# Two attention layers with expert layers: f32r scores one head at a time become bf16 scores two heads at a time, in the two row halves of the array

## The reference

```python
s = jnp.einsum('bhqd,bhkd->bhqk', q, k) * scale      # 16 heads of 8 features
s = jnp.where(causal, s, -jnp.inf)                   # layer 0 only
p = jax.nn.softmax(s, axis=-1)
o = jnp.einsum('bhqk,bhkd->bhqd', p, v)
...
x = _layernorm(x + _L0_attn_ref(...))                # 16 heads, causal
x = _layernorm(x + _L0_ffn_ref(...))                 # 8 experts, top 2, relu
x = _layernorm(x + _L1_attn_ref(...))                # 16 heads, full
x = _layernorm(x + _L1_ffn_ref(...))                 # 15 experts, top 3, gelu, and a shared expert
```

## Time and profile before

| what | value |
|---|---|
| median of three runs | 1208.55 us |
| runs | 1205.19 to 1209.41 us |
| span of the profiled execution | 1058.9 us |
| outside the span, median less span | 149.65 us |
| mean granted clock of TensorE | 0.927 |
| PE, DVE, ACT, POOL busy | 906.3, 679.9, 549.4, 444.0 us |

### The profile page before, as it was taken

How to read it: one execution, slowest core, us unless ns; L and a number is a source line. 1 busy time by engine, 2 the same in 40 slices (tenths; PEclk the granted TensorE clock), 3 DMA queues, 4 the chain that set the end, 5 groups by cost and what they waited for, 6 DMA issues and landing times.

```text
span 1058.9 us, 23206 instructions
## 1 busy us (share of the span) xinstructions
PE 906.3 (86%) x7486; PEld 763.1 (72%) x7486; DVE 679.9 (64%) x2209; ACT 549.4 (52%) x1320; POOL 444.0 (42%) x688
## 2 busy tenths in 40 slices
PE   5899988995999996998999896899898999789910
PEld 4788878884899985766888665676666789688810
DVE  3467755673644475987655566888875565378863
ACT  1356654562655564666766474567556655334300
POOL 7000100054500075477200375325776157377774
PEclk9699998997999998999999897999989999989965
DMA  4557564555468433364667333323444789888421
GB/s 78 103 107 193 114 142 101 135 135 133 106 178 204 125 68 59 53 125 85 144 182 191 66 57 58 51 35 56 87 90 130 216 264 326 280 247 270 122 64 53
DMA packets 111752, 138.49 MB, mean 131 GB/s; under 512 B 12275, under 2 KB 86033, under 8 KB 111633
## 3 DMA queue, kind: packets, MB, share of 16 engines
q1 hardware_dynamic: 100241, 114.97, 45.9%
q0 software_dynamic: 10240, 20.99, 7.9%
q10 hardware_dynamic: 1152, 1.05, 0.6%
HBM read 70.25 MB, written 42.48 MB: 106 GB/s over the span
## 4 chain that ended last, share of the span: by engine, by line
PE 49%; DMA 20%; issue 8%; POOL 7%; DVE 7%; SPq 6%; ACT 2%; POOLq 0%; ACTq 0%; DVEq 0%
DMA QK<-parts 10%; PE bank_O L1132 5%; PE bank_N L1224 5%; DMA G<-yd,ypos 5%; PE bank_FH L1212 4%; POOL xs L877 4%; PE bank_S L1087 4%; PE bank_T L1110 3%; PE bank_S L1083 3%; PE bank_S L1085 3%; PE bank_T L1114 3%; SPq L736 2%; PE bank_T L1112 2%; PE bank_M L1056 2%; DMA QK<-mrow 2%
## 5 line engine op out<-in xcount | busy, mean ns | idle before, releaser
L1298 DVE TENSOR_REDUCE mp<-bank_S 128x3 f32<-128x384 f32 (+1 forms) x512 | 304.2, 620 | 133.9 <-PE bank_S L1087 91.7
L948 ACT ACTIVATE P<-bank_T 128x384 f32<-128x384 f32 (+1 forms) x512 | 260.9, 543 | 90.0 <-PE bank_T L1114 58.2
L891 POOL DMA_INDIRECT G<-yd,ypos x160 | 155.2, 970 | 76.1 <-issue 47.3
L877 POOL DMA_INDIRECT xs<-X,ypos x160 | 155.9, 974 | 48.7 <-issue 43.6
L1132 PE MATMUL bank_O<-P,V 128*32 128x256 f32 (+1 forms) x2048 | 128.8, 371 | 1.4 <-ACT P L948 1.0
L1083 PE MATMUL bank_S<-QK 96*128 96x256 f32 x512 | 112.4, 322 | 18.5 <-DMA QK<-parts 8.9
L1110 PE MATMUL bank_T<-QK 128*128 128x256 f32 x512 | 110.8, 322 | 10.6 <-ACT P L948 6.1
L828 POOL TENSOR_TENSOR rstd<-mv,half 128x2 f32<-128x2 f32 x48 | 9.6, 200 | 261.4 <-DVE mv L1351 261.1
L1085 PE MATMUL bank_S<-rmat 128*128 128x256 f32 x256 | 91.7, 358 | 22.3 <-DMA QK<-parts 21.6
L1083 PEld LDWEIGHTS bank_S<-QK 96*128 96x128 f32 x512 | 79.5, 201 | 35.8 <-DVE mp L1298 20.5
L1087 PE MATMUL bank_S<-QK 96*128 96x128 f32 (+1 forms) x512 | 104.7, 292 | 0.0
(11 more groups left out here) (171 smaller groups left out, 1753.3 us busy)
## 6 DMA issues: line engine op xcount, KB each, us to landing
QK<-parts SPq DMA_DIRECT2D x192, 128.0 KB
QK<-wtab SPq DMA_DIRECT2D x76, 257.0 KB, 3.9
W<-w_in SPq DMA_DIRECT2D x46, 321.0 KB, 4.0
QK<-xs SPq DMA_DIRECT2D x38, 256.0 KB, 4.3
yd<-P SPq DMA_DIRECT2D x38, 256.0 KB, 3.9
xs<-zeros SPq DMA_DIRECT2D x17, 512.0 KB, 8.1
xp<-xs SPq DMA_DIRECT2D x22, 256.0 KB, 4.1
yd<-yb SPq DMA_DIRECT2D x22, 256.0 KB, 4.0
```

Of the source, the lines that this page charges most:

```text
L877: pool.indirect_dma_start(xs[g % 2], bass.IndirectOffsetOnAxis(ypos[L][:, 2 * b + blk, k:k + 1], 0), X[:, 2 * b + blk, :], None).then_inc( ...
L891: pool.indirect_dma_start(G[i][:, blk, k, :], None, yd[g], bass.IndirectOffsetOnAxis(ypos[L][:, 2 * b + blk, k:k + 1], 0))\
L948: act.activation(P[:, (h // 4) % 2, h % 4, 0:n], bank[("T0", "T1")[h % 2]][:, 0:n], ACT.Exp, scale=SCALE)\
L1298: dve.tensor_reduce(mp[:, a % 2, 0:n, h], bank[("S0", "S1")[h % 2]][:, 0:n * w] .rearrange("p (a c) -> p a c", a=n), AX.X, ALU.max).then_i ...
```

## The change

**Three bf16 parts.** q and k are split into a high, a middle and a low bf16 part. `qk_lo` becomes `qk_rest` (DVE), `qk_mid` (ACT) and `qk_low` (DVE). A head's six products of parts take 6 x 8 = 48 rows, so a head fits into half of the array's rows. `spread_parts` writes `parts` to a DRAM buffer `stk` (one DMA), and `stack` reads from it into `QK` with six DMAs for all 16 heads. `QK` is bf16 and holds four attentions; before, its four slots held eight heads each.

**Pairs.** Even heads lie in rows 0 to 63, odd heads in rows 64 to 127. `scores` and `scores_T` issue the matmuls of two heads by turns, one in each row half, each half to a bank of its own. S0 and S1 are now filled together by one pair, and one `row_max` (two heads) frees both; the same for T0 and T1 with one `exp`. The mask is added with four bf16 matmuls of 64 rows for a pair.

**Bursts of eight.** `weigh_V` takes eight heads, four column groups with two heads each, summed in the same bank with 18 columns, of which nine are zero for each head. `O_T` has four transposes in place of eight. `max_neg`, `max_T` and `max_rows` work once for 16 heads in place of twice, and the maxima are split into three bf16 parts.

**Buffers and order.** P holds 16 heads; layer 1's pages store from the same ring of four as layer 0's. `PRM` has other numbers throughout, so that the order of all engines differs. `lay_out()` counts 0.1 more on PE whenever the kind of row or column grouping changes from one step to the next.

The core of the diff:

```diff
+TILING = {"scores": 1, "scores_T": 1, "weigh_V": 2}
+SWITCH = 0.1
...
-        QK = [sb(f"QK{i}", [D, NH // 2, 2, T], F32R) for i in range(4)]
-        VPAD = NH * VW + 32 - VW
-        V = [sb(f"V{i}", [D, 2, VPAD]) for i in range(3)]
-        P = sb("P", [D, 2, 4, 2 * T])
...
+        QK = sb("QK", [D, NQK, 2, NP, T], BF16)
+        V = [sb(f"V{i}", [D, 2, VW // 2 + NH * VW]) for i in range(3)]
+        P = sb("P", [D, PSLOTS, 2 * T])
...
-            def stack(a, u):
-                c = 2 * a + u
+            def spread_parts(a):
                 sp.wait_ge(lo_done.sem, lo_done.all(a))
-                if a < 2:
-                    sp.wait_ge(cleared.sem, 1 + 3 * c)
-                    if c == 0:
-                        sp.wait_ge(cleared_dve.sem, 2)
+                if a >= 2:
+                    sp.wait_ge(stacked[(a - 2) % NQK].sem, stacked[0].all((a - 2) // NQK))
+                sp.dma_start(stk[a % 2].rearrange("i p t -> p i t"), slots(parts[:, :, :, :])).then_inc(spread[a % 2].sem, DMA)
+
+            def stack(a):
+                sp.wait_ge(spread[a % 2].sem, spread[a % 2].all(a // 2))
+                if a < NQK:
+                    sp.wait_ge(cleared.sem, 2 * a + 2)
                 else:
-                    sp.wait_ge(st_ps.sem, st_ps.at(a - 2, 8 * u + 8))
-                p = parts[64 * u:64 * u + 64, :, :, :].bitcast(F32).rearrange("p s i t -> p (s i) t")
-                for i, pair in enumerate((p[:, 0::2, :], p[:, 0::3, :], p[:, 1:3, :])):
-                    sp.dma_start(QK[c % 4][HD * i:HD * i + HD, :, :, :].bitcast(F32), pair).then_inc(stacked[c % 4].sem, DMA)
+                    sp.wait_ge(st_ps.sem, st_ps.all(a - NQK))
+                parts_of = stk[a % 2].rearrange("i (d h) t -> i d (h t)", h=NH)
+                for lane in range(2):
+                    run = parts_of[:, :, lane * NP * T:(lane + 1) * NP * T]
+                    for row, n, src in ((0, 3, run.rearrange("i d c -> (i d) c").rearrange("(s r) c -> r s c", s=2)),
+                                        (3, 2, run.rearrange("(m i) d c -> (i d) m c", m=3)[:, 0::2, :]),
+                                        (5, 1, run.rearrange("i d c -> d i c")[:, 0::5, :])):
+                        at = lane * HALF + row * HD
+                        sp.dma_start(QK[at:at + n * HD, a % NQK, :, :, :].rearrange("r s h t -> r s (h t)"), src)\
+                            .then_inc(stacked[a % NQK].sem, DMA)
...
+            def qk_mid(a):
+                act.wait_ge(rest_done.sem, rest_done.all(a))
+                act.activation(slots(parts[:, :, :, :])[:, 1::3, :], rest[:, :, :], ACT.Copy).then_inc(mid_done.sem, 1)
...
+            def max_rows(a):
+                act.wait_ge(m_kept.sem, m_kept.all(a))
+                for lane in range(2):
+                    at = lane * HALF + QROWS
+                    act.dma_start(QK[at:at + 3, a % NQK, 0, :, :], mrow[3 * NP * lane:3 * NP * (lane + 1), a % 2, :])\
+                        .then_inc(m_stacked[a % NQK].sem, DMA)
...
+            def exp(a, p):
+                act.wait_ge(st_ps.sem, st_ps.at(a, p + 1))
+                if NH * a + 2 * p >= PSLOTS:
+                    _, before, u = before_pair(a, p)
+                    act.wait_ge(o_ps.sem, o_ps.at(before, u + 1))
                 n = 3 * D if a < NB else 2 * T
-                act.activation(P[:, (h // 4) % 2, h % 4, 0:n], bank[("T0", "T1")[h % 2]][:, 0:n], ACT.Exp, scale=SCALE)\
+                i = p_slot(a, 2 * p)
+                act.activation(P[:, i:i + 2, 0:n], pair["T"][:, :].rearrange("p (h c) -> p h c", h=2)[:, :, 0:n], ACT.Exp, scale=SCALE)\
                     .then_inc(exped.sem, 1)
...
+            def mask(banks, which):
+                for i in range(2):
+                    m = masks[which][i]
+                    n = D if which == i else HALF
+                    at = 0 if which == i or i == 0 else HALF
+                    for lane in range(2):
+                        rows = slice(lane * HALF, (lane + 1) * HALF)
+                        pe.matmul(diagonal(banks[lane])[:, :, at:at + n], pick[i][rows, :],
+                                  m[rows, :].unsqueeze(1).broadcast_to((HALF, 2, n)), start=(i == 0), stop=False,
+                                  skip_group_check=True)
+
+            def scores(a, p):
+                banks = free("S0"), free("S1")
+                if a == 0 and p == 0:
+                    pe.wait_ge(const_in.sem, CONST_LOADS * DMA)
+                if p == 0:
+                    pe.wait_ge(stacked[a % NQK].sem, stacked[a % NQK].all(a // NQK))
+                if a < NB:
+                    mask(banks, 0)
+                for qb, (o, n) in enumerate(((0, T), (T, T)) if a >= NB else ((0, D), (D, T))):
+                    for lane in range(2):
+                        rows = slice(lane * HALF, lane * HALF + QROWS)
+                        m = pe.matmul(banks[lane][:, o:o + n], QK[rows, a % NQK, 0, p, qb * D:(qb + 1) * D], QK[rows, a % NQK, 1, p, 0:n],
+                                      start=(a >= NB), stop=(a >= NB or qb == 1), skip_group_check=True)
                 m.then_inc(s_ps.sem, 1)
-                held[k] = maxed.sem, maxed.at(a, h + 1)
-
-            def max_T(a, u):
+                held["S0"] = held["S1"] = maxed.sem, maxed.at(a, p + 1)
...
+            def scores_T(a, p):
+                banks = free("T0"), free("T1")
+                if p == 0:
+                    pe.wait_ge(m_stacked[a % NQK].sem, m_stacked[a % NQK].all(a // NQK))
+                if a < NB:
+                    mask(banks, 1)
+                for kb, (o, n) in enumerate(((0, T), (T, T)) if a >= NB else ((0, T), (T, D))):
+                    for lane in range(2):
+                        rows = slice(lane * HALF, lane * HALF + QROWS + 3)
+                        m = pe.matmul(banks[lane][:, o:o + n], QK[rows, a % NQK, 1, p, kb * D:(kb + 1) * D], QK[rows, a % NQK, 0, p, T - n:T],
+                                      start=(a >= NB), stop=(a >= NB or kb == 1), skip_group_check=True)
                 m.then_inc(st_ps.sem, 1)
-                held[k] = exped.sem, exped.at(a, h + 1)
-
-            def weigh_V(a, g):
+                held["T0"] = held["T1"] = exped.sem, exped.at(a, p + 1)
...
                 for kb in range(2):
-                    for j in range(4):
-                        h = 4 * g + j
-                        w = V[a % 3][:, kb, h * VW:h * VW + 32]
-                        if a >= NB or kb == 0:
-                            o, x = O[32 * j:32 * j + 32, 0:T], P[:, g % 2, j, kb * T:(kb + 1) * T]
-                        else:
-                            o, x = O[32 * j:32 * j + 32, D:T], P[:, g % 2, j, T:T + D]
-                        m = pe.matmul(o, w, x, start=(kb == 0), stop=(kb == 1), skip_group_check=True)
+                    for lane in range(2):
+                        for j in range(BURST // 2):
+                            h = BURST * u + 2 * j + lane
+                            w = V[a % 3][:, kb, h * VW + (VW // 2 if lane == 0 else 0):][:, 0:VW]
+                            q = 0 if a >= NB else kb * D
+                            x = P[:, p_slot(a, h), kb * T:kb * T + T - q]
+                            m = pe.matmul(O[32 * j:32 * j + VW, q:T], w, x, start=(kb == 0 and lane == 0), stop=(kb == 1 and lane == 1),
+                                          skip_group_check=True)
                 m.then_inc(o_ps.sem, 1)
-                held["O"] = o_kept.sem, o_kept.at(a, g + 1)
-
-            def O_T(a, blk):
+                held["O"] = o_kept.sem, o_kept.at(a, u + 1)
...
+            def qk_low(a):
+                dve.wait_ge(mid_done.sem, mid_done.all(a))
+                p = slots(parts[:, :, :, :])
+                dve.tensor_tensor(p[:, 2:4, :], rest[:, :, :], p[:, 1::3, :], ALU.subtract).then_inc(lo_done.sem, 1)
+
+            def row_max(a, p):
+                dve.wait_ge(s_ps.sem, s_ps.at(a, p + 1))
+                if p == 0 and a >= 2:
+                    dve.wait_ge(mT_ps.sem, mT_ps.all(a - 2))
                 n, w = (3, D) if a < NB else (2, T)
-                dve.tensor_reduce(mp[:, a % 2, 0:n, h], bank[("S0", "S1")[h % 2]][:, 0:n * w]
-                                  .rearrange("p (a c) -> p a c", a=n), AX.X, ALU.max).then_inc(maxed.sem, 1)
-
-            def max_neg(a, u):
-                heads = slice(8 * u, 8 * u + 8)
-                top = mp[:, a % 2, 0:2, heads]
-                dve.wait_ge(maxed.sem, maxed.at(a, 8 * u + 8))
+                S = pair["S"][:, :].rearrange("p (r c) -> p r c", r=2)[:, :, 0:n * w].rearrange("p r (a c) -> p r a c", a=n)
+                dve.tensor_reduce(mp[:, a % 2, 0:n, :, 0, p].rearrange("p a r -> p r a"), S, AX.X, ALU.max, negate=True)\
+                    .then_inc(maxed.sem, 1)
...
+                dve.tensor_tensor(mid, neg, top_half(neg), ALU.subtract).then_inc(m_hi.sem, 1)
+                dve.wait_ge(m_hi.sem, m_hi.all(a))
```

(1 more changed line is left out.)

428 lines of the change are left out of this document (199 added, 229 removed), and 17 rows, old and new, of the table PRM.

## The result

The changed kernel takes 1193.2 us (four runs, 1188.23 to 1194.88) against 1208.36 for the kernel before (1205.19 to 1209.41): ratio 0.985, interval 0.980 to 0.989. It is faster by 15 us, or 1.5%; 140 us were predicted, and 1193 lies outside the range of 1010 to 1155.

What follows compares the result with a forecast made beforehand. The prediction took TensorE to bound layer 0's attention and no engine to be full in layer 1's. Scores to 667 us plus an unchanged 251 gave a span of 918, with 150 outside 1068 us, range 1010 to 1155.

Steps and rivals of the forecast that it cites:

- The sum: Whole kernel, added along the scores rounds: span 918 us, with 150 outside it 1068, saving 140.
- Outside the span: Whole kernel: 149.65 us lie outside the profiled span of 1058.9 and stay, making up the median.
- TensorE's rate: Scores matmuls: both row halves run at once, a pair 0.37 us in layer 0, 0.25 in layer 1; 153 us less work.
- The first rival: Scores matmuls: row halves run one after another, so no gain, about 1205 us; chance 8%.
- the rival that drains for 0.22: TensorE: each change of grouping drains it, up to 0.22 us instead of 0.08, giving 1113 us; chance 10%.
- Hand-off and bare stretches: Scores to row_max: lost double buffer binds only where scores stand alone, 14 pairs a layer at 1.65 and 1.76 us.
- the second rival: Scores to row_max: the hand-off decides, a round in layer 0 takes 2.8 us against 2.38, giving 1265; chance 11%.
- Pace in layer 0: Layer 0's other 114 pairs: 1.90 us each, TensorE's need of 1.71 at nine tenths, together 217 us up to 262.
- Without scores: Between the layers' scores: 46 us of TensorE work and 9 for layer 1's first stack, 55 in all.
- Layer 1: Layer 1's scores: last 114 pairs at 2.6 us, VectorE's 2.12 over 0.82, plus 15 for pages and gathers; 336 in all.
- Tail: From the last row_max to the end of the span: unchanged at 251 us.
- The fourth rival: TensorE: gaps at each hand-off lower its granted clock to 0.8, 75 us more work, half on the path, 1105; chance 5%.

Runs made afterwards that it cites:

- before_again: The kernel before, unedited, run and profiled once more: 1211.5 us, ratio 1.001.
- experiment 5: Changed kernel with each pair's matmuls issued head by head: 1027.1 us (0.974); with row maxima also taken by head: 1022.8 (0.971), beside 1024.2 for the changed kernel.
- after: The changed kernel, unedited, in its first measurement and profile: 1193.2 us, ratio 0.985 to the kernel before.
- after_third: The changed kernel, unedited, on a chip where the kernel before took 1054.4 us: 1024.2 us, ratio 0.970.
- experiment 7: Changed kernel with four more bf16 matmuls a pair in the last eight attentions (filler): 1210.4 us (0.985); with scores matmuls issued twice instead: 1263.4 (1.029).
- sets 1, 4 and 5: Groups of runs, each on one chip, with the kernel before run beside: its medians were 1212.4, 1222.8 and 1219.0 us.
- set 6: Group of runs on one chip with POOL pauses behind the indirect DMAs; the kernel before took 1207.2 us beside them.

## Why the prediction was wrong

The sum was a span of 918 and 149.65 outside it. Measured are a span of 1028 without late results and 165 more with them. So the 125 us by which 1068 is too low are 110 in the span and 15 in what stood for the disturbance.

**Outside the span.** The step "The sum is against the span of 1058.9, which with the 149.65 is the median by construction" failed. The median and the profile came from two kinds of execution; the difference lies inside the span, in the stretches in which POOL scatters and gathers. That it was nearly right as a constant is luck: before pays 1217.8 - 1058.9 = 159, after 1192.4 - 1027.9 = 165. What it hid was the largest loss in both kernels.

**TensorE's rate.** Right. A pair of `scores_T` in layer 0 takes 162.85 - 162.51 = 0.34 us, 0.37 predicted: both halves at once. The first rival is dead. A change of grouping costs 163.28 - 163.02 - 0.17 = 0.09 us, 0.08 predicted; the rival that drains for 0.22 is dead too. The Trainium skill's page "TensorEngine Tiling (Array Packing)", Key Properties, says that a change of the tiling mode drains TensorE, without a size; this 0.09 us agrees with a short drain. `weigh_V` with eight heads takes 162.51 - 161.08 = 1.43 us there; 2 x 0.63 + 0.16 = 1.42 was the estimate.

**Hand-off and bare stretches.** The mechanism was right, and in layer 0 the price was right at full clock; that TensorE would have full clock there was the error. The first rounds of `after` (`scores` alone), with two windows of that stretch (columns as in the earlier trace rows):

```profile
24.54 0.34 PE L1115 MATMUL pair_S<-bmat 64*128 64x256 bf16 x4 [1.15 <-DVE mp L1347]
...
26.19 0.34 PE L1115 MATMUL pair_S<-bmat 64*128 64x256 bf16 x4 [1.14 <-DVE mp L1347]
...
27.84 0.51 PE L1115 MATMUL pair_S<-bmat 64*128 64x256 bf16 x4 [1.14 <-DVE mp L1347]
...
29.81 0.50 PE L1115 MATMUL pair_S<-bmat 64*128 64x256 bf16 x4 [1.15 <-DVE mp L1347]
```

```profile
23.30:26.60 3.30, 1.01 (x18) 0.62 (x16) 3.07 (x4) 0.63 (x1) 0.00 (x0) 1.00 0.82 132
26.80:33.40 6.60, 4.41 (x28) 2.45 (x28) 2.81 (x3) 0.60 (x1) 0.00 (x0) 0.50 0.98 271
```

A round takes 26.19 - 24.54 = 1.65 us at a granted clock of 1.00 (1.62 predicted) and 29.81 - 27.84 = 1.97 at 0.50, which is 1.2 GHz. In `after_third` most of the first rounds take 1.97, and where layer 1 begins they take 2.02, where 1.76 was predicted:

```profile
25.06 0.50 PE L1115 MATMUL pair_S<-bmat 64*128 64x256 bf16 x4 [1.15 <-DVE mp L1347]
...
27.03 0.50 PE L1115 MATMUL pair_S<-bmat 64*128 64x256 bf16 x4 [1.14 <-DVE mp L1347]
...
402.68 0.61 PE L1130 MATMUL pair_S<-QK 48*128 48x256 bf16 x4 [1.41 <-DVE mp L1347]
404.70 0.61 PE L1130 MATMUL pair_S<-QK 48*128 48x256 bf16 x4 [1.41 <-DVE mp L1347]
```

```profile
397.00:425.00 28.00, 10.77 (x64) 3.91 (x66) 23.19 (x46) 2.87 (x5) 22.04 (x31) 0.50 0.74 169
```

TensorE stands still for 1.1 to 1.4 us of each round. One thing about the record: in `after_third` it holds no granted clock before 60.9 us, and a window there reads 1.00; the durations say half clock until there (`qk` takes 2.07 us at 31.71 and 1.13 at 159.03). The sum also left out that three of layer 0's first rounds hold a `qk` and take 2.76 us. The two stretches of 14 rounds come to some 30 and 29 us, 11 us over my sum. The loss by the hand-off is small (experiment 5): the second rival, slower at 1265, is dead too.

**Pace in layer 0.** This step failed most, 46 us: predicted 1.90 a pair, "PE's 1.71 at nine tenths". Three windows of `after_third`: all engines, first a mixed stretch, then one in which the clock was 1.00 throughout, and `row_max` in the latter:

```profile
50.00:150.00 100.00, 84.93 (x1160) 55.94 (x1160) 66.69 (x166) 52.06 (x92) 7.96 (x28) 0.90 0.64 169
...
71.30:115.50 44.20, 36.66 (x574) 25.30 (x574) 34.92 (x90) 26.86 (x49) 5.51 (x18) 1.00 0.58 146
...
71.30:115.50 44.20, 20.00 (x21) 1.00 0.58 146
```

At full clock 21 pairs take 44.2 us, 2.10 each. TensorE's need was right, 36.66/21 = 1.75 us a pair against 1.71; the "nine tenths" was not: it was busy for 83% of the stretch, with VectorE at 79%, so neither is full. Of TensorE's 7.5 us without work, 2.8 ended with an `exp`, 2.1 with a `row_max`, 1.4 with the load of `xT`. Over the whole 50 to 150 us the pace is 2.17 (46 pairs), because parts of it ran at half clock: the first 11 us, by the durations, and 20 of the recorded 89. TensorE, no longer full, stood still between its steps and was also clocked lower; both made the 46 us, and their shares were not separated.

**Without scores.** 76 us in place of 55: I had 46 us of TensorE's work without a gap, and 9 for the first `stack`; the work took 62 us, at a clock of 0.90, with 14 us of gaps.

**Layer 1.** 359 in place of 336. The last 64 pairs (592.8 to 755.5) took 163 us, 2.54 each, as predicted (2.6), but before they took 163.5 too (644.7 to 808.2). The window of before, then that of `after_third`:

```profile
645.00:808.00 163.00, 146.22 (x1214) 110.99 (x1214) 132.41 (x423) 102.48 (x236) 91.70 (x152) 0.94 0.39 72
```

```profile
593.00:755.00 162.00, 129.09 (x1254) 66.74 (x1254) 131.72 (x350) 98.38 (x166) 81.18 (x141) 0.82 0.37 81
```

The 2.6 came true, but not for its reason: VectorE was to need 0.16 us less a pair, and it was busy 132.41/64 = 2.07 us a pair before and 131.72/64 = 2.06 after. TensorE's share fell from 90 to 80% although its clock fell from 0.94 to 0.82; VectorE's stayed at 81%. So TensorE did not set the pace here, and the filler (experiment 7) found room on it; that VectorE and the fixed order do is argued, not shown. The error lies in the first half, with pages and gathers in it: 196 us where I had 155 + 15.

**Tail.** "The last 251 us as they are" failed: 272, with the clock at 0.85 in place of 0.88 and page work in another order; which of the two was not tried. With late results it is 357.

**The clock.** The fourth rival had 5%, and its state came about: 0.877 without late results, 0.816 with them, where it named 0.8. By my sum of the clock record, TensorE is at half clock for 256 us in `after_third` against 157 in the first profile of before, and with late results for 441 in `after` against 323 in `before_again`. The 0.877 and the 256 leave out the first 61 us of `after_third`, which have no record and ran at half clock; with its first 24 us counted so too, before would have 180, and `after_third` 317. The low clock did not come alone, as the rival had it, but with each loss above; how much of the 110 us is its own stays open.

**What POOL does to TensorE.** Between a set with late results and one without them the changed kernel differs by some 180 us with indirect DMAs (about 0.985 x 1222.8 = 1204 against 1024) and by nothing without them (963.8 and 963.9). The Trainium skill's page "SBUF — State Buffer", section "SBUF: two separate sides", says that on the engines' side only the pair of ports that VectorE and GpSimd share causes contention, and that TensorE never waits on anyone. By that alone POOL's work in SBUF should leave TensorE untouched. In every traced kernel of sets 1, 4 and 5 that has indirect DMAs and no pauses, between 71 and 82 waits ended on "remote" beside them, 270 to 370 us in all; of set 6 only paced kernels were traced, and the kernel before took 1207 us there. So something between TensorE and its waiters is held up, but no run shows whether a port is the cause, and so whether the page's rule is touched at all. Nor does a run show whether TensorE stops or only its signals arrive late, or whether the state belongs to the chip or to the set: only sets 4 and 5 share a chip, and both have it.

## What to carry to other kernels

Before a profile is used for a sum, its span must be near the measured time: a gap of 150 us is a sign that the profile shows another kind of execution, and one more profile settles it. Work taken from the fullest engine comes back only as far as the next engine, the order and the clock allow; here TensorE's busy time fell by 99 us (906.3 to 807.7, at a lower clock), and 30 us were gained. Where "remote" ends long waits, look at what else runs just then: 0.33 us of POOL's time behind each indirect DMA brought 87 us where the change brought 15. A count of late signals should be held against waits that really ended late, since a missing record looks like a late one.

## What the runs showed of the hardware

- In sets 1, 4 and 5 waits of up to 27 us for TensorE's results ended late while POOL issued indirect DMAs every 1.26 us, the longest in layer 1's attention within 3 us after unbroken runs of 17. Plain DMAs from POOL (0.55 us each) do nothing of the kind (set 5). A pause of 0.33 us behind each indirect DMA cuts the longest such wait to 5.5 us and recovers 87 of some 165 us; one of 0.54 us leaves 8 us of such waits in all.
- Matmuls in rows 0 to 63 and in rows 64 to 127 overlap even when four of one half are listed ahead of four of the other: 0.35 us for 768 columns in each half, as when they alternate (0.34).
- In a stretch in which TensorE works for 0.6 us and stands still for 1.4, it is granted half its clock throughout (0.50 in 397 to 425 us of `after_third`). In the first rounds of layer 0 the same round takes 1.65 us at full clock and 1.97 at half (`after`).
